# Layer 1 of a two-layer graph attention kernel: where TensorE meets the softmax, when the first one-hots are made, and in which order the first tile is divided

## The reference

```
for (W, q, k, b, heads) in ((W1, q1, k1, b1, 4), (W2, q2, k2, b2, 1)):
    xr    = einsum('nd,rdf->rnf', x, W)                 # 3 relations
    qi    = xr[etype, dst] @ q;  kj = xr[etype, src] @ k
    alpha = leaky_relu(qi + kj, 0.2)
    e     = exp(alpha - segment_max(alpha, dst)[dst])
    z     = segment_sum(e, dst)
    out   = segment_sum(e / (z[dst] + 1e-16) * xr[etype, src], dst) + b
    x     = elu(out)                                    # after the first layer only
result = layernorm(input + out)
```

## Time and profile before

| | |
|---|---|
| runs | 2635.74, 2637.34, 2642.82 us, median 2637.34 |
| the profiled execution | 2640.77 us, its span 2639.0 us |
| mean granted clock of TensorE | 0.988 of full |
| busy, share of the span | PE 97%, POOL 65%, ACT 43%, DVE 39% |
| dense products of layer 1 | from 165 to 773 us |
| sums of layer 1 | from 784 to 1364 us |

### The profile page before, as it was taken

One profiled execution on the slowest core, in us unless ns is written; L12 is line 12 of the kernel. 1 busy time (PEld: TensorE's weight loads), 2 busy tenths in 40 slices (PEclk: granted clock), 3 DMA queues, 4 the chain that ended last, 5 costly groups with the idle time before them and its releaser, 6 DMA issues.

```text
span 2639.0 us, 45100 instructions
## 1 busy us (share of the span) xinstructions
PE 2552.3 (97%) x10749; PEld 1771.1 (67%) x10749; DVE 1040.1 (39%) x2057; ACT 1142.1 (43%) x3156; POOL 1726.3 (65%) x1797
## 2 busy tenths in 40 slices
PE   7999999999979999999988999999998999999998
PEld 7765555555559999999986555555554555555554
DVE  9520401222158888888886010000002233222332
ACT  2321111111129999999976111111111566665564
POOL 1257777777527777777744777777770677777675
PEclk9999999999989999999999999999999999999999
DMA  6662243323329999999953432222222999999997
GB/s 203 184 168 58 60 120 84 84 72 84 84 80 324 314 318 314 318 313 319 307 195 98 112 96 85 71 65 63 66 65 73 315 321 320 325 321 326 312 331 256
DMA packets 163285, 503.02 MB, mean 191 GB/s; under 512 B 59455, under 2 KB 59862, under 8 KB 162702
## 3 DMA queue, kind: packets, MB, share of 16 engines
q0 software_dynamic: 99696, 353.91, 40.7%
q1 hardware_dynamic: 55104, 144.46, 17.2%
q10 hardware_dynamic: 8396, 3.49, 0.6%
HBM read 414.42 MB, written 87.24 MB: 190 GB/s over the span
## 4 chain that ended last, share of the span: by engine, by line
PE 91%; DVE 3%; DMA 3%; issue 1%; POOL 1%; ACT 1%; ACTq 0%; DVEq 0%; SPq 0%; POOLq 0%
PE banks L638 43%; PE banks L747 22%; PE banks L770 10%; PE banks L766 10%; PE banks L543 2%; PE banks L509 2%; DMA ring<-xr_table,row_idx 2%; DVE ring L1184 1%; PE banks L559 1%; POOL ring L1142 1%; PE banks L659 1%; PE banks L530 1%; DMA qkw<-in_L_gnn_k 0%; DMA ring<-in_x 0%; DVE big L1423 0%
## 5 line engine op out<-in xcount | busy, mean ns | idle before, releaser
L638 PE MATMUL banks<-work 128*125 128x384 f32 x3600 | 1175.5, 487 | 1.3 <-DVEq L1320 1.3
L1142 POOL DMA_INDIRECT ring<-xr_table,row_idx x880 | 833.6, 947 | 371.2 <-PE banks L770 146.6
L638 PEld LDWEIGHTS banks<-work 128*125 128x125 f32 x3600 | 673.1, 188 | 473.9 <-issue 4.4
L1120 POOL DMA_INDIRECT big<-k_table,row_idx x830 | 798.7, 962 | 254.4 <-issue 242.0
L898 ACT COPY ring<-banks 125x384 f32<-125x384 f32 x300 | 143.9, 480 | 1050.1 <-PE banks L638 1050.1
L747 PE MATMUL banks<-ring,work 128*125 128x193 f32 x3520 | 579.6, 327 | 6.9 <-ACT work L926 6.9
L747 PEld LDWEIGHTS banks<-ring,work 128*125 128x125 f32 x3520 | 579.3, 187 | 7.1 <-issue 7.1
L926 ACT ACTIVATE work<-work,wE 128x125 f32<-128x125 f32 x1760 | 548.8, 388 | 35.8 <-DVE work L1466 22.9
L1481 DVE TENSOR_TENSOR big<-big,banks 125x772 f32 x440 | 421.6, 958 | 70.2 <-PE banks L747 52.0
L766 PE MATMUL banks<-ring,work 128*125 128x384 f32 x880 | 359.5, 490 | 15.4 <-DMA ring<-xr_table,row_idx 15.1
L770 PE MATMUL banks<-ring,work 128*125 128x386 f32 x880 | 360.9, 492 | 0.0
(11 more groups left out here) (221 smaller groups left out, 918.2 us busy)
## 6 DMA issues: line engine op xcount, KB each, us to landing
xr_table<-ring SPq DMA_DIRECT2D x75, 337.8 KB
xr_table<-ring SPq DMA_DIRECT2D x75, 336.9 KB
x_turned<-work SPq DMA_DIRECT2D x40, 375.0 KB, 3.5
work<-x_turned SPq DMA_DIRECT2D x40, 375.0 KB, 4.1
ring<-xr_table,row_idx POOLq DMA_INDIRECT x880, 5.1
work<-in_L_gnn_W SPq DMA_DIRECT2D x36, 384.0 KB, 6.3
big<-k_table,row_idx POOLq DMA_INDIRECT x830, 2.4
work<-in_x SPq DMA_DIRECT2D x26, 336.0 KB
```

The costliest lines, as they stand in the source:

```text
L638: last = pe.matmul(bank[u % DBANKS][0:TN, 0:n_cols], xT_slot(k, TN)[:, c, :], w_cols(r, first, n_cols)[:, c, :], start=(c == 0), stop=(c = ...
L1120: nc.gpsimd.indirect_dma_start(k_at(l, st), None, ktab[l], bass.IndirectOffsetOnAxis(ap=row_idx[:, st:st + 1], axis=0)).then_inc(s["k_gath ...
L1142: nc.gpsimd.indirect_dma_start(ring[:, st % GS, 0:ROWW[l]], None, xrtab[l], bass.IndirectOffsetOnAxis(ap=row_idx[:, st:st + 1], axis=0)).t ...
```

## The change

It has three parts, all in layer 1.

1. TensorE's eight meetings with the softmax stand after other units: before after (18, 0), (18, 1), (18, 2), (18, 3), (18, 5), (19, 0), (19, 2) and (19, 3), now after (17, 4), (17, 5), (18, 0), (18, 1), (18, 3), (18, 4), (19, 1) and (19, 2). Layer 2's places stay as they were.
2. VectorE makes the four first one-hots ahead of the copies of the weights, and waits for the last dense unit before them. Its clearing of a part of `big` stays behind `w_ready`.
3. The addition to `brow` moves from the end of the sums to their start, behind the clearing. At the end the constant and the reciprocal are applied to the first tile's sums of weights alone, then this tile is divided, then the other 24 tiles' reciprocals are taken, then tile 1 is divided.

```diff
--- before.py
+++ after.py
@@ -718,7 +718,7 @@
                 meets = [lambda c=c: turn_k(c) for c in range(RC)]
                 meets += [lambda f=f, w=w: f(w) for w in range(2) for f in (turn_ends, turn_carry)]
                 if H > 1:
-                    spots = [(18, 0), (18, 1), (18, 2), (18, 3), (18, 5), (19, 0), (19, 2), (19, 3)]
+                    spots = [(17, 4), (17, 5), (18, 0), (18, 1), (18, 3), (18, 4), (19, 1), (19, 2)]
                 else:
                     meets.append(lambda: turn_e(0))
                     spots = [(17, 4), (17, 5), (18, 0), (18, 1), (18, 2), (18, 3), (18, 5), (19, 0), (19, 2)]
@@ -1445,6 +1445,17 @@
                     for h in range(H):
                         link(scan(h, c_in[:, h:h + 1]))
                 nc.vector.tensor_tensor(al, al, amax[:, 0:H, :], ALU.subtract).then_inc(s["diff_ready"], 1)
+                if l == 0:
+                    dve.wait_ge(s["dense_done"], UNITS * (NT + 2))
+
+                    def one_hot(st, slot):
+
+                        dve.wait_ge(s["S_built"], st + 1)
+                        nc.vector.tensor_scalar(hot[:, slot, :], iota_n[:, :], dloc[:, bass.ds(st, 1)], None, ALU.is_equal
+                                                ).then_inc(s["hot_built"], 1)
+
+                    for j in range(AHEAD):
+                        one_hot(j, j)
                 for h in range(H):
                     dve.wait_ge(s["e_turned"], HM * l + h + 1)
                     link(nc.vector.tensor_copy(wE[:, 0:STEPS, h].rearrange("p (r c) -> p c r", c=RC),
@@ -1458,16 +1469,8 @@
                 if l == 0:
                     nc.vector.memset(big[0:TN, AMAX_AT:K_AT], 0.0).then_inc(s["sums_zeroed"], 1)
                     dve.sem_inc(s["sum_added"], AHEAD)
-                    dve.wait_ge(s["dense_done"], UNITS * (NT + 2))
-
-                    def one_hot(st, slot):
-
-                        dve.wait_ge(s["S_built"], st + 1)
-                        nc.vector.tensor_scalar(hot[:, slot, :], iota_n[:, :], dloc[:, bass.ds(st, 1)], None, ALU.is_equal
-                                                ).then_inc(s["hot_built"], 1)
-
-                    for j in range(AHEAD):
-                        one_hot(j, j)
+                    dve.wait_ge(s["brow_loaded"], 16 * (l + 1))
+                    link(nc.vector.tensor_scalar(brow[0:TN, :], brow[0:TN, :], 1.0, None, ALU.add))
                     dve.wait_ge(s["sums_zeroed"], 4)
                     with dve.Fori(0, STEPS // GS) as i:
                         for j in range(GS):
@@ -1484,13 +1487,15 @@
 
                     dve.wait_ge(s["sum_added"], AHEAD + STEPS)
                     z = small[0:TN, c_z][:, 0:NT * H]
-                    link(nc.vector.tensor_scalar(z.rearrange("p (t h) -> p t h", h=H),
-                                                 big[0:TN, 0:NT * RWL].rearrange("p (t h w) -> p t h w", t=NT, h=H)[:, :, :, D // H],
-                                                 SOFTMAX_EPS, None, ALU.add))
-                    link(nc.vector.reciprocal(z, z))
-                    dve.wait_ge(s["brow_loaded"], 16 * (l + 1))
-
-                    link(nc.vector.tensor_scalar(brow[0:TN, :], brow[0:TN, :], 1.0, None, ALU.add))
+
+                    def weights_sums(a, b):
+                        link(nc.vector.tensor_scalar(z[:, a * H:b * H].rearrange("p (t h) -> p t h", h=H),
+                                                     big[0:TN, a * RWL:b * RWL].rearrange("p (t h w) -> p t h w", t=b - a, h=H
+                                                                                          )[:, :, :, D // H],
+                                                     SOFTMAX_EPS, None, ALU.add))
+                        link(nc.vector.reciprocal(z[:, a * H:b * H], z[:, a * H:b * H]))
+
+                    weights_sums(0, 1)
 
                     def divide(t, add):
 
@@ -1503,6 +1508,7 @@
 
                     dve.sem_inc(s["h_ready"], 2)
                     divide(0, brow[0:TN, :]).then_inc(s["u_ready"], 1)
+                    weights_sums(1, NT)
                     divide(1, brow[0:TN, :]).then_inc(s["u_ready"], 1)
                     for i, last_turn in turns(dve, NT, U):
                         for k in range(U):
```

## The result

The changed kernel took 2646.34 us (median of 19 runs), the kernel before 2641.60 (median of 19 beside it): ratio 1.0018, 95% interval 1.0011 to 1.0025, so +4.7 us (+2.9 to +6.6): slower, by less than the 0.3% that the prediction counts as a change. Forecast: +3.5 us. The profiled execution took 2647.47 us with a span of 2645.8.

What follows compares the result with a forecast made beforehand. The prediction took TensorE to bound the kernel almost throughout (dense 43%, layer 1's sums 22%). It summed +5.7 - 1.8 + 0 - 0.4 = +3.5 us, making 2640.8 us on the median, range 2635.5 to 2647.

Steps and rivals of the forecast that it cites:

- The mechanism of part 1: Behind unit (17, 5): turn_k(1) waits for VectorE's k addition, tied to the last W2 load, so TensorE stops, then runs slow.
- The stop: TensorE standing still between unit (17, 5) and turn_k(1): 10.3 us, with 9.8 to 10.9 from the load's landings.
- The slow clock behind it: First dense unit after TensorE's stop at turn_k(1): 2.1 us lost to the low clock, bounds 1.7 to 3.7.
- The end of the dense products: Last dense unit of layer 1: ends 5.7 us later, stops removed 6.7, added 12.4.
- ScalarE's copy: Copy of the last dense unit: no longer behind the exponential, so it starts 0.2 us after that unit, not 1.7.
- The first sum's matmul: Start of layer 1's sums: released by the gather at 788.1 against 784.21, +3.9 us, bounds +3.4 to +4.1.
- The landing itself: First gather of layer 1's sums: lands 4.7 us after its issue, from a span of 4.2 to 4.9.
- The way through the weights: From turning the exponentials to ScalarE's first scalings: ready at 786.1, 2 us before the gather lands at 788.1.
- rival C: Start of the sums: gather lands sooner, the weights' way ends last, +1.5 us in all, 2638.8 us; chance 8%.
- Part 2: Earlier one-hots at the start of the sums: hidden behind the gather, worth 0; alone 0.1 to 0.8 us.
- Nothing: 0: Clearing (1.76) and brow addition (0.57) ahead of VectorE's fifth one-hot: cost 0, at most 0.5 us if late.
- Part 3: End of layer 1: brow addition leaves the path, 0.71 us, two small instructions return 0.3: -0.4, bounds -0.1 to -0.7.

Runs made afterwards that it cites:

- e1: The kernel before with part 1 alone (the spots): ratio 1.0045 to the kernel before, which took 3017 us beside it.
- e5: The changed kernel with GpSimd clearing that part of the sums and the brow addition ahead of the W2 products: 2644.51 us, ratio 1.0012 to the kernel before.
- e7: The changed kernel with the brow addition alone back at the end of the sums, the clearing staying at their start: ratio 1.0002 to the kernel before.
- e8: The changed kernel itself, unaltered, run again: ratio 1.0016 to the kernel before.
- e9: The changed kernel with a wait for the clearing's end ahead of the brow addition: ratio 1.0014 to the kernel before.
- e10: The kernel before with part 1 alone, run once more: ratio 1.0035 to the kernel before, five runs only.
- e3: The changed kernel with the second and third relation's W2 loads issued ahead of a tile's stores: ratio 0.9985 to the kernel before, which took 3017 us.
- e6: The changed kernel with e5's clean start of the sums and e3's earlier W2 loads: 2630.54 us, ratio 0.9960 to the kernel before.
- e11: The changed kernel with part 1 undone (parts 2 and 3 alone), run once more: ratio 1.0008 to the kernel before.
- e2: The changed kernel with part 1 undone (parts 2 and 3 alone): ratio 1.0012 to the kernel before, which took 3017 us beside it.
- e12: The kernel before with only the last two meetings one unit later, at (19, 3) and (19, 4): ratio 1.0011 to the kernel before.
- e4: The kernel before with e3's earlier W2 loads, all spots as before: ratio 0.9995 to the kernel before, which took 3017 us.

## Why the prediction was right, and where it was not

**The mechanism of part 1 was right.** The stop was worked out at 10.3 us and measured at 10.00, and at 9.7 to 9.9 in e1, e5, e7, e8, e9 and e10. Moving the load alone takes it away (e3 against the changed kernel, e6 against e5). The slow clock behind it was put at 2.1; the distance from turn_k(1) to turn_k(2), 4.3 at full clock, was 6.0, 6.1, 6.7, 7.0, 7.0, 7.1 and 7.1 in the seven traces: 1.7 to 2.8.

**The end of the dense products:** +5.7 expected; from the end of (17, 4) 65.8 us against 60.9, +4.9, and +5.8 in e8; the stop was 0.3 shorter than forecast and the slow unit behind it 0.4. **ScalarE's copy** came free as worked out: 3.6 us from its end to the gather's issue in both.

**The first sum's matmul:** +3.9 expected, +2.3 measured and +3.2 in e8. It came 4.1 us behind the gather's issue, not 4.7, and 4.0 to 4.2 in all seven traces with early one-hots at this speed. The landing itself, which the trace of the changed kernel lists for its first gather, is 3.9 us, below every landing that the prediction had; the 4.9 of the earlier trace rows was listed for the stretch and not for the first gather, and I took it for being nearest by line. The way through the weights was ready about 1.3 us sooner (788.79 + 1.40 = 790.19), not 2, so rival C was not reached.

**Part 2 is the step that failed, in the sentence "Nothing: 0".** I asked whether VectorE's clearing and addition would be late for the sums, and they weren't. I did not ask whom they run beside. The addition stands right behind the clearing without a wait, and GpSimd is at its first gathers there. The third gather of the kernel before, 1.66 us long while the one-hots stood behind the clearing, was the sign of it in the trace that I had. The cost is 1.7 us, against a gain of 1.1 to 1.2 at the first sum's matmul (e11, e2), where the prediction had 0.1 to 0.8 for the part alone.

The Trainium skill (SBUF — State Buffer, "Who interferes with whom") says that a VectorE operation such as tensor_scalar can take a pair of ports that GpSimd needs, and shuts it out for the whole instruction; the section "SBUF: two separate sides" says that a DMA issued by GpSimd then starves for its descriptors. By the first of these sections of the Trainium skill a clearing, which reads nothing, is harmless. The runs agree: 0.95 with the clearing alone (e7), 3.25 with the addition behind it. The runs also say that the addition held the gather up ahead of its own start, from about when it was queued: the gather of the changed kernel, issued at 788.66, would have ended at 789.61, 0.98 us before the addition began. e9 against the changed kernel is the evidence for that reading, with e12 beside it; that it goes by the ports is not shown, since they are in no trace.

**Part 3:** -0.4 expected, -0.2 measured. The two small instructions took 0.17 and 0.18, and 0.54 with their hand-overs (1375.18 to 1375.72), where I had counted 0.3. That the first tile's earlier division brings nothing was right: line 1521 follows the divisions of line 1504 on VectorE without idle time.

**The size.** +3.5 against +4.7. By the profiled execution: first sum's matmul 1.6 too high, the sums 3.0 too low. Of the 3.0 the hold is 1.7; the rest fits that execution's clock, 0.56 over 10 us from the first sum's matmul on against 0.85 in e8, which took 1.4 us less for the same sums. So two errors of opposite sign made the total closer than its terms, and that is luck. The forecast's 2640.8 us stood on the median of three runs, 2637.34; beside the changed kernel the kernel before took 2641.60, so of the 5.5 us between 2640.8 and 2646.34 only 1.2 are the change's.

**The version that beats both** is e6: 2630.54 us, ratio 0.9960, -10.3 us. Its rows show all three points at once, no idle time ahead of turn_k(1), a second gather of 0.95, the first sum's matmul 62.2 us from turn_k(0):

```profile
719.67 0.60 PE L700 MATMUL banks<-ident,big 128*110 128x128 f32 x4
...
774.82 0.95 POOL L1150 DMA_INDIRECT ring<-xr_table,row_idx  x1 [0.30 <-issue]
...
777.54 2.93 PE L753 MATMUL banks<-ring,work 128*125 128x193 f32 x8 [6.00 <-DMA ring<-xr_table,row_idx]
```

That is 9.5 us ahead of the kernel before's 71.7. The spots of the change are right once the load no longer stands behind the stores: with W2 sooner the first sum's matmul comes 62.0 us from the end of (17, 4) with them (e3) and 69.5 with the old ones (e4).

## What to carry to other kernels

Before a meeting of two engines is moved forward, follow the other engine's program back to the first thing it waits for, and ask whether that moves too: here a load stood behind the very unit that had been covering it. A filled stop on the busiest engine is worth nothing while the chain runs through another (e12). And ask of every operation that is moved which engines work beside it at the new place, not only who waits for it; put a wait between a long operation and one that shuts GpSimd out, or move the second away (e9 and e7; the gain of that wait is in the traces, not in the whole times).

## What the runs showed of the hardware

- A brow addition of 0.50 us on VectorE, queued behind a clearing of 1.76 us, lengthened a GpSimd gather's issue from 0.95 us to between 3.23 and 3.26 in five executions of three kernels; waited for first, by 0.17 us; the clearing alone, by nothing. The one-hots behind the clearing lengthened the third gather to 1.65 to 1.66 us where it was issued 0.7 us ahead of them, and to 2.08 where it was issued 1.11 ahead (before and e12).
- The low clock after a stop is a matter of the execution. The same unit, in two programs that are alike up to there (before and e12), took 4.4 or 6.1 us from turn to turn behind a stop of 1.9 us, and over 10 us from the first sum's matmul on the mean clock was 0.56 in one execution and 0.85 in another of the same kernel.
- Beside e1 to e4 the kernel before took 3017 us in place of 2640, with stops on all engines. In e1 ScalarE's copies kept their mean of 480 ns, and the dense matmuls had 504 ns in place of 487. The cause is not known. The record gives the same chip number for these runs as for e5 to e8, beside which it took 2640.88 us, so it need not be a property of one chip.
